# Layer 0's experts beside layer 1's attention: first-batch work moved between turns, stacks issued in pieces

## The reference, cut to what matters

```python
# layer 0: causal attention with l2-normalised heads, residual, then 16 experts, top 2
probs = softmax(xt @ Wr + br); w, idx = top_k(probs, 2); w = w / sum(w)
h = gelu(einsum('td,edh->teh', xt, W1) + b1)       # 16 experts, 128 -> 256 -> 128
y = xt + einsum('teo,te->to', einsum('teh,eho->teo', h, W2) + b2, comb)
# layer 1: attention with 16 query heads and 4 key heads of 8, full softmax, then 8 experts, top 1
q, k = q * rf, k * rf                              # rotary factors
attn = softmax(einsum('brkqa,bkca->brkqc', q5, k) / sqrt(128))
s = einsum('brkqc,bkca->brkqa', attn, v);  o = s @ w_o;  out = s + o
```

## Time and profile before

| | us |
|---|---|
| median of 3 runs | 1641.16 |
| lowest and highest | 1639.39 and 1644.71 |
| the profiled execution, its own time | 1643.79 |
| its span in the trace | 1642.1 |
| PE busy (share of the span) | 1455.0 (89%) |
| DVE busy | 1173.7 (71%) |
| ACT busy | 944.5 (58%) |
| POOL busy | 833.3 (51%) |

### The profile page before, as it was taken

How to read it: one execution, slowest core, us unless ns; L and a number is a source line. 1 busy time by engine, 2 the same in 40 slices (tenths; PEclk the granted TensorE clock), 3 DMA queues, 4 the chain that set the end, 5 groups by cost and what they waited for, 6 DMA issues and landing times. The chain is left out here.

```text
span 1642.1 us, 29856 instructions
## 1 busy us (share of the span) xinstructions
PE 1455.0 (89%) x9492; PEld 720.0 (44%) x9492; DVE 1173.7 (71%) x3136; ACT 944.5 (58%) x1805; POOL 833.3 (51%) x926
## 2 busy tenths in 40 slices
PE   3999999979985668999999999999999999849996
PEld 1444444459984312333333323333333332239996
DVE  3688777746432667899989998899989998514443
ACT  2565565524442256777777777777777777712221
POOL 4688888740332246556555565556555520114443
PEclk9999999879998889999999999999999999969998
DMA  1111221169987021142211221122211210347771
GB/s 39 46 56 54 63 64 41 62 214 303 314 240 219 25 67 34 60 126 75 62 57 54 78 61 54 59 73 75 61 57 57 70 53 11 108 164 237 237 240 56
DMA packets 134183, 165.23 MB, mean 101 GB/s; under 512 B 20292, under 2 KB 106436, under 8 KB 131532
## 3 DMA queue, kind: packets, MB, share of 16 engines
q1 hardware_dynamic: 103356, 84.72, 17.4%
q10 hardware_dynamic: 16848, 48.13, 9.1%
q0 software_dynamic: 13824, 30.47, 5.9%
HBM read 115.88 MB, written 51.04 MB: 102 GB/s over the span
## 5 line engine op out<-in xcount | busy, mean ns | idle before, releaser
L1692 DVE TENSOR_REDUCE c_mx<-c_ps_mx 128x1 f32<-128x512 f32 x1024 | 650.8, 684 | 93.8 <-PE c_ps_mx L1953 87.5
L1559 ACT ACTIVATE pt<-c_ps_e 128x512 f32<-128x512 f32 x1024 | 567.0, 601 | 198.8 <-PE c_ps_e L1927 187.3
L1927 PE MATMUL c_ps_e<-c_qst,c_kex 74*128 74x512 bf16 (+1 forms) x1024 | 345.7, 386 | 3.8 <-ACT pt L1559 2.2
L1940 PE MATMUL c_ps_v<-pt,c_vp 128*32 128x512 f32 x2048 | 274.5, 608 | 1.1 <-ACT pt L1559 0.7
L1953 PE MATMUL c_ps_mx<-c_kex,c_qst 64*128 64x512 bf16 x1024 | 201.0, 389 | 62.9 <-DVE c_mx L1692 47.4
L1377 POOL DMA_INDIRECT c_gy<-ys,c_rows x128 | 123.9, 968 | 224.2 <-PE c_ps_v L1940 108.4
L1953 PEld LDWEIGHTS c_ps_mx<-c_kex,c_qst 64*128 64x128 bf16 x1024 | 49.2, 93 | 367.9 <-DVE c_mx L1692 347.1
L559 ACT ACTIVATE a_pt<-a_ps_s,temp 128x1024 f32<-128x1024 f32 (+3 forms) x128 | 113.0, 884 | 95.9 <-PE a_ps_s L653 93.5
L500 POOL DMA_INDIRECT xs<-a_xn,meta x128 | 136.1, 1063 | 37.4 <-issue 34.6
L1470 POOL DMA_INDIRECT rows<-c_row,c_bsl x64 | 63.8, 997 | 160.0 <-PE c_ps_v L1940 129.0
L1646 ACT ACTIVATE f_h<-c_ps_e,pt 128x256 f32<-128x256 f32 x160 | 67.4, 470 | 123.2 <-PE c_ps_e L2102 123.2
(11 more groups left out here) (243 smaller groups left out, 2141.3 us busy)
## 6 DMA issues: line engine op xcount, KB each, us to landing
pt<-in_we ACTq DMA_DIRECT2D x80, 321.0 KB, 4.5
f_w<-in_we ACTq DMA_DIRECT2D x37, 576.0 KB, 3.8
c_qst<-qparts SPq DMA_DIRECT2D x80, 192.0 KB
f_x<-rows SPq DMA_DIRECT2D x40, 257.0 KB, 3.8
pt<-xs SPq DMA_DIRECT2D x80, 128.0 KB, 4.7
ys<-f_y SPq DMA_DIRECT2D x80, 128.0 KB, 4.3
qparts<-c_qp SPq DMA_DIRECT2D x16, 384.0 KB, 2.6
x<-in_x SPq DMA_DIRECT2D x16, 256.0 KB, 2.9
```

The lines of the kernel that those rows point to most:

```text
L1559: nc.scalar.activation(pt[:, s % 4, hl, :], ps_e[:, e_bank(64 * b + n)], ACT.Exp, scale=QSCALE).then_inc(exp_done, 1)
L1692: nc.vector.tensor_reduce(mx[:, g % 2, col:col + 1], ps_mx[:, m_bank(64 * b + 2 * m + par)], AX, ALU.max).then_inc(mx_done, 1)
L1927: nc.tensor.matmul(ps_e[:, e_bank(64 * b + n)], kex[rows, p, k_head(hl), kt * P:(kt + 1) * P], qst[rows, p, q_head(g, hl), :], start=True, ...
L1940: last = nc.tensor.matmul(ps_v[32 * hl:32 * (hl + 1), :], vp[:, p, kt, hl, :], pt[:, s % 4, hl, :], start=kt == 0, stop=kt == NT - 1)
```

## The change

- **End of block 1.** `zero_tails` takes a list of experts: SP issues the first eight, ACT the other eight in batch 7, two behind its second exponential, two behind its third, four behind its fourth. `transpose_rows` on PE stands behind the second value product instead of the first, and `place_rows` on DVE behind `add_output` of the batch before instead of in front of it.
- **Turns 44 to 58.** Statistics and moments of batch 0 are in turn 44 (from 45 and 46). Its normalised rows are made on DVE in turn 47 instead of on POOL. PE transposes them in turn 48 (from 49), projects both pairs of token tiles in turn 49 (from 50 and 51), the second into a free bank of `ps_mx`, and transposes k and q in turn 51 (from 55 and 56), q into another free bank. ACT's copies stand in turns 48, 49, 51 and 52.
- **Stacks of batch 0.** `load(0, 2)` moves from turn 56 to 50, `put_k` from 58 to 53, `put_q` from 60 to 55. The seven transfers of `k_stack` go out two a turn in turns 56 to 58 and one in 59; the seven of `q_stack` one in turn 59 and two a turn in 60 to 62. Before, all seven of the one stood in turn 61 and all seven of the other in 62.
- **Maxima.** FIRST is 67 instead of 69, and DVE does both reductions of a pair ahead of `f_down`.
- **End of the turns.** Statistics, moments and the first shifts of batch 1 and batch 0 stand in turns 75, 76 and 77 (from 79 and behind the turns), SP's first shift in turn 78. ACT does one exponential of a spare column behind the turns.
- **Body of batch 0.** SP issues four of the seven `q_stack` transfers ahead of `shift(i, o, 2)`, ACT the other three behind step 5. On POOL two gathers for batch 2 instead of four stand ahead of `k_parts` and `q_parts` of batch 1.

```diff
-FIRST = 69
+FIRST = 67
...
-                        gt.zero_tails(sp)
+                        gt.zero_tails(sp, range(0, E0 // 2))
...
+                    if not nxt:
+                        gt.zero_tails(act, range(E0 // 2, E0 // 2 + 2))
                     exps(b, 2)
...
+                    if not nxt:
+                        gt.zero_tails(act, range(E0 // 2 + 2, E0 // 2 + 4))
                     exps(b, 3)
...
+                    if not nxt:
+                        gt.zero_tails(act, range(E0 // 2 + 4, E0))
                     exps(b, 4)
...
                         k_stack(sp, i, o + 1)
+                        q_stack(sp, i, o + 1, range(4))
                         shift(i, o, 2)
-                        q_stack(i, o + 1)
...
+                    if 56 <= j < 59:
+                        k_stack(sp, 0, 0, range(2 * (j - 56), 2 * (j - 55)))
+                    if j == 59:
+                        k_stack(sp, 0, 0, (6,))
+                        q_stack(sp, 0, 0, (0,))
+                    if 60 <= j < 63:
+                        q_stack(sp, 0, 0, range(2 * (j - 60) + 1, 2 * (j - 59) + 1))
+                    if j == 78:
+                        shift(0, 0, 0)
...
-                gather(0, 2, range(0, NT))
+                gather(0, 2, range(0, 2))
                 k_parts(pc, 0, 1)
                 q_parts(pc, 0, 1)
-                gather(0, 2, range(NT, 2 * NT))
+                gather(0, 2, range(2, 2 * NT))
...
+                        if s == 5 and not prev:
+                            q_stack(act, i, o + 1, range(4, 7))
...
+                nc.scalar.activation(warm[:], k.temp[:, 1:2], ACT.Exp)
                 xT_copy(0, 1)
...
-                    for par in halves:
+                    for par in range(2):
...
+                    if j == 47:
+                        dve.wait_ge(rstd_ready, 1)
+                        for t in range(NT):
+                            last = nc.vector.tensor_scalar(xn[:, 0, t, :], x1[:, 0, t, :], mv[:, t, 0:1], rstd[:, t:t + 1],
+                                                           ALU.subtract, ALU.mult)
+                        last.then_inc(xn_ready, 1)
...
-                    if j > FIRST:
-                        row_max(0, 0, j - FIRST - 1, (1,))
-                    if j == 79:
-                        shifts(0, 0, 0)
-                    if j == 79:
-                        statistics(0, 1)
+                    if j == 75:
+                        statistics(0, 1)
+                    if j == 76:
+                        moments(0, 1)
+                    if j == 77:
+                        shifts(0, 0, 0)
...
                     if j > FIRST:
-                        row_max(0, 0, j - FIRST - 1, (0,))
+                        row_max(0, 0, j - FIRST - 1)
                     f_down(j)
...
+                    if j == 48:
+                        free = x_rows(free, 0, 0)
                     if j == 49:
-                        free = x_rows(free, 0, 0)
-                    if j in (50, 51):
-                        free = project(free, 0, 0, j - 50)
-                    if j == 55:
+                        project(free, 0, 0, 0)
+                        free = project(free, 0, 0, 1, ps_mx[:, 0])
+                    if j == 51:
                         free = k_columns(free, 0, 0)
-                    if j == 56:
-                        free = q_columns(free, 0, 0)
+                        q_columns((prj_sb, NT), 0, 0, ps_mx[:, 1])
```

More of the change, by code:

```diff
@@ L712, in _ @@
                     values(b, 1)
+                    if not nxt:
+                        gt.transpose_rows(pe, ps_p)
                     if nxt2:
@@ L1217, in experts0_and_attention1, with k_stack @@
         with nc.Block() as block:
-            def k_stack(eng, i, o):
+            def k_stack(eng, i, o, pieces=range(7)):
                 b, h, p = batch(i, o)
[L1222 to L1226, removed]
+                if pieces[0] == 0:
+                    if not (isinstance(b, int) and b < 2):
+                        eng.wait_ge(s_ps, 64 * (b - 1))
+                        eng.wait_ge(mx_ps, 32 * (b - 1))
+                    eng.wait_ge(k_out[p], 16 * (h + 1))
+                for n in pieces:
+                    par, a = n // 3 % 2, n % 3
@@ L1227, in k_stack @@
                     base, cols = P // 2 * par, slice(par * KV1 // 2, (par + 1) * KV1 // 2)
+                    if n == 6:
+                        base, par, cols = 0, 1, slice(KV1 // 2, KV1)
                     parts = kparts_d[p].rearrange("j (d c) l -> d j c l", d=DH1)[:, :, cols, :].rearrange("d j c l -> d j (c l)")
[L1229 to L1231 removed]
@@ L1232, in k_stack @@
[L1232 to L1236, removed]
+                    if n == 6:
+                        row, count, src = 0, DH1, parts.rearrange("d j m -> j d m")[2]
+                    elif a < 2:
+                        row, count, src = base + PART * a, PART, parts
+                    else:
+                        row, count, src = base + 2 * PART, (3 - par) * DH1, parts.rearrange("d j m -> j d m")[0:3 - par]
@@ new lines, in k_stack, with q_stack @@
+                    eng.dma_start(kex[row:row + count, p, cols].rearrange("r c l -> r (c l)"), src).then_inc(k_in[p], 16)
+            def q_stack(eng, i, o, pieces=range(7)):
+                b, h, p = batch(i, o)
+                if pieces[0] in (0, 4):
+                    eng.wait_ge(q_out[p], 16 * (h + 1))
+                for n in pieces:
+                    par, a = (1, 2) if n == 6 else (n // 3, n % 3)
+                    base, cols = P // 2 * par, slice(par * H1 // 2, (par + 1) * H1 // 2)
+                    part = qparts_d[p, a].rearrange("(d c) l -> d c l", d=DH1)[:, cols, :].rearrange("d c l -> d (c l)")
+                    if n == 6:
+                        row, count, src = 0, DH1, part
+                    elif a < 2:
+                        row, count, src = base + PART * a, PART, part.unsqueeze(1).to_broadcast([DH1, 3, H1 // 2 * L])
+                    else:
+                        row, count, src = base + 2 * PART, (3 - par) * DH1, part.unsqueeze(0).to_broadcast([3 - par, DH1, H1 // 2 * L])
+                    eng.dma_start(qst[row:row + count, p, cols].rearrange("r c l -> r (c l)"), src).then_inc(q_in[p], 16)
@@ L1973, in x_rows, with project @@
                     return xT_sb, b + 1
-                def project(free, i, o, pair):
+                def project(free, i, o, pair, out=ps_j):
                     b, h, p = batch(i, o)
@@ L1990, in k_columns, with q_columns @@
                     return kT_sb, b + 1
-                def q_columns(free, i, o):
+                def q_columns(free, i, o, out=ps_j):
                     b, h, p = batch(i, o)
```

83 lines of the change are left out of this document (28 added, 55 removed).

## The result

The changed kernel takes 1612.2 us (median of four runs, 1611.4 to 1615.1) against 1641.2 for the kernel before; the estimated ratio is 0.9818, 95% interval 0.9802 to 0.9835. A second series of it gave 1611.6 and 0.9819 (0.9803 to 0.9835). The forecast was 1612 with a range of 1601 to 1624. One execution in each of three series came out far longer (2339.7, 2060.3 and 2304.9 us) and is left out of all medians here.

A forecast was written before the change was run, and what follows sets the result against it. The prediction took the expert turns as bound by TensorE with DMA right behind, plus stops. Its terms, 2.0 + 4.7 + 2.8 + 15 + 1.0 + 3.3 = 28.8 us off 1643.79, gave 1615.0, or 1612 for the median; range 1601 to 1624.

The forecast's parts named there:

- End of block 1: End of block 1: sharing zero blocks between SP and ACT lets ACT finish sooner, 2.0 us saved, bounds 0 and 3.3.
- Turns 44 to 58: Batch 0's work in the turns: four TensorE waits go, less 0.5 us for statistics and moments; 4.7 us saved.
- Stacks of batch 0: Late turns: stack transfers begun earlier and spread over seven turns cut TensorE's wait from 14.3 to 11.5; 2.8 us saved.
- Maxima: Turns with maxima: both reductions ahead of `f_down` make a turn 2.5 instead of 3.63; 15 us saved, bounds 11 and 18.
- Table load: Behind the turns: ACT's 1.28 us table load moves into its idle time; 1.0 us saved, bounds 0 and 1.3.
- First body: Body of batch 0: batch 1's query stack starts 2.75 us earlier, on two queues; 3.3 us saved, bounds 0 and 5.
- The stack is hidden: Rival for batch 0's stacks: seven turns and eight buffers absorb them, wait falls from 14.3 to 3; 1604 us, chance 0.18.
- DMA binds the turns: Rival: savings of turns 44 to 58 return as stack wait, maxima turns hold at 3.0; 1626 us, chance 0.10.
- ACT pays at both ends: Rival: zero blocks stop ACT's exponentials, and its three stack transfers in the body speed up nothing; 1618 us, chance 0.12.

The follow-up runs named there:

- Without `warm`: The changed kernel without the one exponential that loads ACT's table behind its last turn: 1615.63 us, ratio 0.9837.
- better spread: The changed kernel with every batch's stack rows reordered so that each query transfer reads contiguous rows, and the split key written three times: 1603.51 us, ratio 0.9766.
- whole stacks: The changed kernel with batch 0's stacks put back, seven key transfers at once in turn 61 and seven query transfers in turn 62: 1612.67 us, ratio 0.9836.
- early stacks: The changed kernel with batch 0's stacks whole but early, key stack in turn 57 and query stack in turn 59: 1616.3 us, ratio 0.9837.

## Why the prediction was right

In the total it was right to 1 us, and its two large steps were right in mechanism. Two of the small ones, the stacks and the first body, were wrong in mechanism and worth little; a third, the table load, stays open.

- *Turns 44 to 58*, forecast 4.7, bounds 3.5 to 5.2: 5.8, shown both ways (115.7 and 121.5). This is above the upper bound. The windows from turn 44 to 58, before and then changed, show why:

```profile
446.02:482.58 36.56, 31.30 (x224) 29.07 (x223) 13.89 (x52) 15.68 (x37) 11.30 (x17) 1.00 0.82 241
```

```profile
439.19:469.93 30.74, 30.60 (x224) 28.92 (x223) 14.92 (x57) 15.80 (x37) 10.45 (x15) 1.00 0.95 281
```

TensorE's idle time fell from 5.26 to 0.14 us: the four waits went, and the statistics cost 0.14 and not 0.5. The same 224 matmul records are also busy for 0.70 us less; the timeline shows the first matmuls behind a stop longer (0.92 and 0.94 us for the four of a projection, 0.84 where none stops), which the forecast had not counted.
- *Stacks of batch 0*, forecast 2.8 from a wait of 11.5: the wait is 10.4, the gain 0.3 in the pair of traces shown, 0.8 against the mean of five, 0.5 by medians, 2.9 by ratios; the size is not settled. The reasoning failed. I took a shorter wait for shorter time and did not look at the clock of the turns in it, though the earlier trace rows showed 0.66 for that stretch.
- *Maxima*, forecast 15: turns at 2.5 (2.48 measured), 30 us from the first pair to that of turn 79 (31.96, 2.1 of them one turn at the low clock), 7.7 behind it (7.46). Undoing the order costs 13.9. Batch 1's sums in turn 75 stop nothing: TensorE waits 0.48 us there once, and the two turns with statistics and shifts take 2.8.
- *Table load*, forecast 1.0: 0 to 1.7. Without `warm` the first exponential comes 1.4 us later; whether the body's stop takes that in is open.
- *First body*, forecast 3.3, lower bound 0: 0.1, within a scatter of 1.5 either way. The stack does leave ahead of the 2.7 us of shifts, and I wrote that the scores that need the shifts "are the ones that wait anyway". They wait for the shifts, 6.81 us.
- *End of block 1*, forecast 2.0: 2.6 by the cuts, 2.3 to 2.9 by the medians. The size is right, but my reason (the store waits for the chain of the last batch alone) holds in one of three traces. In the other two SP's queue held the store. Nor did ACT's fifth exponential come sooner than in the kernel before: it starts 12.4 us behind the last-but-one reciprocal instead of 11.5.
- *The rivals.* "The stack is hidden" (1604) is wrong: 10.4 us of waiting stay, and 7.0 even where it is better spread. "DMA binds the turns" is wrong: turn savings stayed. "ACT pays at both ends" is half right: the two queues gained nothing, but the zero blocks on ACT did not undo the gain at the end of block 1.

Put together, with the table load and the first body at 0, 2.6 + 5.8 + 16.5 (turn 58 to the first scores: 87.0 to 70.5) = 24.9, against 29.0 and 29.9 between the medians of the two series. Against the forecast's 28.8 the terms lose 4.3 in the table load and the first body and 1.3 in stacks and maxima together, and win 1.7 in the two others. The 4 to 5 us between them no edit explains. The start (turn 1) is 4.4 earlier in the mean of the eleven traces with the zero blocks split than in the three without, 1.8 more than the 2.6 counted; the rest is not settled. That the total came out to 1 us was partly luck.

## What to carry to other kernels

Before moving a late transfer, look at the DMA share to the end of the wait for it: if it is low there, change the transfer's shape (which dimension is slowest) before its place. A shorter wait is not yet shorter time; compare the busy time of the same instructions in the stretch. Where an engine waits once a turn for another's second instruction, look for the instruction between the two that need not be there.

## What was not expected

- What follows a stop runs at the low clock, so a stop broken in two slows two turns: turn 67 with its pair took 4.58 us (501.02 to 505.60) at a granted clock of 0.50, the turns from 508.51 on 2.47. With whole stacks turn 67 took the same 4.58 (501.00 to 505.58); with pieces the matmuls of the turn before it, 494.78 to 498.88, ran at 0.50 too.
- SP itself stalls in the issue behind a stack. In the kernel with early stacks the issue of a store that takes 0.47 us elsewhere took 5.49 (4.54 at 505.92 in the kernel before); why is not shown:

```profile
489.26 5.49 SPq L1327 DMA_DIRECT2D ys<-f_y  x1
```
